# Two DMA queues for the first weights, and own orders of work for the first two steps of a graph-network kernel

## The reference

```python
def layer(h, adj, Wl, bl, Ws, bs, Wr, br, g, beta):
    u = einsum('bid,bjd->bij', h, h) / sqrt(384)
    delta = softmax(u) * adj
    attn = delta / (sum(delta, -1) + 1e-10)
    ctx = (attn above diagonal) @ (h @ Wl.T + bl) \
        + diag(attn) * (h @ Ws.T + bs) \
        + (attn below diagonal) @ (h @ Wr.T + br)
    return relu(layernorm(ctx, eps=1e-12) * g + beta)

h = relu(layernorm(x, 1e-5)); x = x + layer2(layer1(h))   # L0: two sublayers
h = relu(layernorm(x, 1e-5)); x = x + layer3(h)           # L1
```

## Time and profile before

| | us |
|---|---|
| median of 3 runs | 1231.8 (1230.98 to 1233.81) |
| the profiled execution | 1233.29 |
| its span | 1231.5 |
| TensorE busy | 1215.2 |
| VectorE busy | 1089.2 |
| ScalarE busy | 833.1 |
| GpSimd busy | 326.8 |

### The profile page before, as it was taken

The page is one execution under the profiler, slowest core; times in us unless marked ns, Lnnn a source line. Parts: engine busy times, 40 slices in busy tenths (PEclk is TensorE's granted clock), DMA queues, the critical chain, the costliest instruction groups (busy, mean ns, idle before and its releaser), DMA issues.

```text
span 1231.5 us, 26747 instructions
## 1 busy us (share of the span) xinstructions
PE 1215.2 (99%) x7163; PEld 1208.6 (98%) x7163; DVE 1089.2 (88%) x3127; ACT 833.1 (68%) x2079; POOL 326.8 (27%) x439
## 2 busy tenths in 40 slices
PE   7899999999999999999999999999999999999997
PEld 6899999999999999999999999999999999999997
DVE  6799888888887799999999999999999999999986
ACT  6577767666666667776766666676666666676764
POOL 1234232222222123321212121232323232323221
PEclk9999999999999999999999999999999999999999
DMA  5444232324232234333333323322332323232321
GB/s 179 135 121 129 89 114 83 118 82 119 83 106 91 94 99 130 116 100 104 96 106 96 107 85 103 129 85 95 97 107 98 106 95 99 96 97 98 99 91 54
DMA packets 112922, 127.18 MB, mean 103 GB/s; under 512 B 11104, under 2 KB 100192, under 8 KB 112864
## 3 DMA queue, kind: packets, MB, share of 16 engines
q1 hardware_dynamic: 112864, 126.50, 32.8%
HBM read 76.91 MB, written 49.55 MB: 103 GB/s over the span
## 4 chain that ended last, share of the span: by engine, by line
PE 97%; DMA 1%; issue 1%; DVE 1%; SPq 0%; ACT 0%; POOLq 0%; POOL 0%; DVEq 0%; ACTq 0%
PE right_bank L448 25%; PE left_bank L448 24%; PE context_bank L448 24%; PE context_bank L479 17%; PE score_bank L423 6%; PE score_bank L431 1%; DMA rows<-weights 1%; DMA nodes<-squares 0%; PE edge_bank L438 0%; ACT side_parts L610 0%; DVE context L872 0%; SPq L340 0%; DVE rows L881 0%; DVE stats L844 0%; DVE turned L744 0%
## 5 line engine op out<-in xcount | busy, mean ns | idle before, releaser
L448 PE MATMUL left_bank<-weight,node_t 128*128 128x384 f32 x1728 | 338.1, 339 | 0.0
L448 PE MATMUL right_bank<-weight,node_t 128*128 128x384 f32 x1728 | 335.0, 338 | 2.2 <-DVE weight L827 2.2
L448 PE MATMUL context_bank<-weight,node_t 128*128 128x384 f32 x1728 | 332.3, 337 | 3.1 <-ACT context_bank L616 3.1
L610 ACT ACTIVATE side_parts<-right_bank 128x384 fp32r<-128x384 f32 x192 | 94.4, 492 | 317.3 <-PE context_bank L479 317.1
L448 PEld LDWEIGHTS context_bank<-weight,node_t 128*128 128x128 f32 x1728 | 303.0, 188 | 3.7 <-ACT context_bank L616 3.4
L448 PEld LDWEIGHTS left_bank<-weight,node_t 128*128 128x128 f32 x1728 | 304.3, 188 | 0.0
L448 PEld LDWEIGHTS right_bank<-weight,node_t 128*128 128x128 f32 x1728 | 299.4, 188 | 3.5 <-issue 2.6
L479 PE MATMUL context_bank<-side_parts,attn_t 128*128 128x386 f32 x1152 | 240.0, 344 | 2.2 <-issue 1.9
L479 PEld LDWEIGHTS context_bank<-side_parts,attn_t 128*128 128x128 f32 x1152 | 198.9, 189 | 4.5 <-issue 3.6
L748 DVE TENSOR_TENSOR node_t<-nodes,node_t 128x768 fp32r<-128x768 f32 x94 | 121.6, 1294 | 18.2 <-ACT node_t L558 18.2
L1034 POOL TENSOR_TENSOR edge_block<-edge,tri 128x512 f32<-128x512 f32 x96 | 131.9, 1374 | 0.0
(11 more groups left out here) (78 smaller groups left out, 1519.6 us busy)
## 6 DMA issues: line engine op xcount, KB each, us to landing
squares<-turned SPq DMA_DIRECT2D x94, 384.0 KB, 2.7
nodes<-squares SPq DMA_DIRECT2D x376, 96.0 KB, 2.2
rows<-x SPq DMA_DIRECT2D x64, 384.0 KB, 3.7
out<-rows SPq DMA_DIRECT2D x31, 384.0 KB, 2.6
adj_in<-adj SPq DMA_DIRECT2D x96, 64.0 KB, 1.9
piece<-weights SPq DMA_DIRECT2D x18, 192.0 KB, 2.5
rows<-weights SPq DMA_DIRECT2D x3, 576.0 KB, 8.5
vector_rows<-vectors SPq DMA_DIRECT2D x3, 384.0 KB, 5.3
```

The source lines that it names most:

```text
L448: mm = nc.tensor.matmul(bank[:, 0:D], node_t[:, s.parity, k, c, a], weight[:, s.phase % 2, w, c, b], start=False, stop=(c, a) == (CH - 1, ...
L610: nc.scalar.activation(side_parts[:, side, HI, 0:D], side_bank[side][k][:, 0:D], ACT.Copy).then_inc(side_hi[side], 1)
```

## The change

SP no longer loads the RIGHT and LEFT weights and biases. ScalarE's queue does, ahead of ScalarE's first computation: the second tile of x(0), chunk 0 of the RIGHT weights with a semaphore of its own, the RIGHT bias, chunks 1 and 2, the LEFT weights, the LEFT bias. SP loads the first tile of x(0), the identity, x(1), the SELF weights, x(2), adj(0), the triangles, the SELF bias. Chunk 0 of RIGHT is split ahead of the first fill_source and input_shift. right(0,0) waits for the low part of tile 0 alone (`first_split`). The fillers are five and five.

In step 0, ScalarE does scale_self, seed_self and copy_cross ahead of the fills; VectorE does context_stats, denominator and sum_scores ahead of turn_nodes(2), and turn_nodes(3) behind centre. Step 1 gets orders of its own on TensorE, ScalarE and VectorE: TensorE does scores(2) after left(1,1) and not after self(1,0); ScalarE does split_nodes(2) after the seeds; VectorE does split_nodes(2) after the norms and turn_nodes(4) after centre(1,0). Step 2 on stays as `body`.

```diff
...
         first_bias_in = [sem("first_left_bias_in"), sem("first_right_bias_in"), sem("first_self_bias_in")]
+        first_x_in = sem("first_x_in")
+        first_chunk_in = sem("first_chunk_in")
...
         first_rounded = sem("first_rounded")
+        first_split = sem("first_split")
...
-            def load_first(w):
-                sp.dma_start(first_raw[:, w * CH:(w + 1) * CH], weights[0, w * CH:(w + 1) * CH].rearrange("c p e -> p c e"))\
-                  .then_inc(first_in[w], 16)
-            def load_first_bias(w):
-                sp.dma_start(vector_row(0, ROW_LEFT + w), vectors[0, ROW_LEFT + w].partition_broadcast(P)).then_inc(first_bias_in[w], 16)
-            load_x(Step(0, 0, 0))
+            sp.dma_start(rows[:, 0], x_pairs[0, :, 0]).then_inc(first_x_in, 16)
             sp.dma_start(context[:, 0, 0:P], identity).then_inc(identity_in, 16)
             load_x(Step(0, 0, 1))
-            for w in (RIGHT, LEFT):
-                load_first_bias(w)
-                load_first(w)
+            sp.dma_start(first_raw[:, SELF * CH:(SELF + 1) * CH], weights[0, SELF * CH:(SELF + 1) * CH].rearrange("c p e -> p c e"))\
+              .then_inc(first_in[SELF], 16)
+            load_x(Step(0, 1, 0))
             load_adj(Step(0, 0, 0))
             sp.dma_start(tri[:, :, :], triangles).then_inc(triangles_in, 16)
-            load_x(Step(0, 1, 0))
-            load_first(SELF)
-            load_first_bias(SELF)
+            sp.dma_start(vector_row(0, ROW_SELF), vectors[0, ROW_SELF].partition_broadcast(P)).then_inc(first_bias_in[SELF], 16)
...
             def project_side(s, k, side, within=None):
-                pe.wait_ge(node_hi, s.n + 1)
-                pe.wait_ge(node_lo, s.n + 1)
+                if isinstance(s.n, int) and (s.n, k, side) == (0, 0, RIGHT):
+                    pe.wait_ge(first_split, 1)
+                else:
+                    pe.wait_ge(node_hi, s.n + 1)
+                    pe.wait_ge(node_lo, s.n + 1)
...
+            def second_step(s):
+                prev, nxt = s.ahead(-1), s.ahead(1)
+                project_side(s, 0, RIGHT)
+                weigh(prev, 1)
+                project_side(s, 0, LEFT)
+                project_self(s, 0)
+                project_side(s, 1, RIGHT)
+                project_side(s, 1, LEFT)
+                scores(nxt)
+                weigh(s, 0)
+                project_self(s, 1, within=lambda: turn_cross(nxt))
             def body(s):
                 if isinstance(s.n, int) and s.n == 0:
                     return first_step(s)
+                if isinstance(s.n, int) and s.n == 1:
+                    return second_step(s)
...
             mm.then_inc(banks_open, 1)
-            keep_busy(3)
+            keep_busy(5)
             pe.wait_ge(ident_rounded, 1)
             start = Step(0, 0, 0)
             transpose_first(start)
-            keep_busy(6)
+            keep_busy(5)
...
-            def split_first(w):
-                act.wait_ge(first_in[w], 16)
-                for i in range(w * CH, (w + 1) * CH):
-                    nc.scalar.activation(piece_part(0, i, HI), first_raw[:, i], ACT.Copy).then_inc(first_hi[w], 1)
+            def split_first(w, chunks=range(CH)):
+                for i in chunks:
+                    act.wait_ge(first_chunk_in if (w, i) == (RIGHT, 0) else first_in[w], 16)
+                    nc.scalar.activation(piece_part(0, w * CH + i, HI), first_raw[:, w * CH + i], ACT.Copy).then_inc(first_hi[w], 1)
+            def load_first(w, chunks, arrived):
+                n = slice(w * CH + chunks[0], w * CH + chunks[-1] + 1)
+                act.dma_start(first_raw[:, n], weights[0, n].rearrange("c p e -> p c e")).then_inc(arrived, 16)
+            def load_first_bias(w):
+                act.dma_start(vector_row(0, ROW_LEFT + w), vectors[0, ROW_LEFT + w].partition_broadcast(P)).then_inc(first_bias_in[w], 16)
...
                 split_edges(s)
+                scale_self(s, 0)
+                seed_self(s, 1)
+                copy_cross(nxt)
+                seed_side(nxt, 0, RIGHT)
                 fill_source(second, 0)
                 fill_source(second, 1)
+                split_side(s, 1, RIGHT)
+                split_side(s, 1, LEFT)
+                scale_self(s, 1)
+                seed_side(nxt, 0, LEFT)
+                exponentials(nxt)
+                fill_source(third, 0)
+                fill_source(third, 1)
+            def second_step(s):
+                nxt, third = s.ahead(1), s.ahead(3)
+                split_side(s, 0, RIGHT)
+                seed_self(s, 0)
+                split_edges(s)
+                split_side(s, 0, LEFT)
+                seed_side(s, 1, RIGHT)
                 scale_self(s, 0)
+                seed_side(s, 1, LEFT)
                 seed_self(s, 1)
+                split_nodes(nxt)
...
                 scale_self(s, 1)
+                exponentials(nxt)
                 seed_side(nxt, 0, LEFT)
-                exponentials(nxt)
...
                     return first_step(s)
+                if isinstance(s.n, int) and s.n == 1:
+                    return second_step(s)
...
+            act.dma_start(rows[:, 1], x_pairs[0, :, 1]).then_inc(x_in[0], 16)
+            load_first(RIGHT, (0,), first_chunk_in)
+            load_first_bias(RIGHT)
+            load_first(RIGHT, (1, 2), first_in[RIGHT])
+            load_first(LEFT, (0, 1, 2), first_in[LEFT])
+            load_first_bias(LEFT)
             act.wait_ge(identity_in, 16)
             nc.scalar.activation(ident_r[:, :], context[:, 0, 0:P], ACT.Copy).then_inc(ident_rounded, 1)
             start = Step(0, 0, 0)
+            split_first(RIGHT, (0,))
             fill_source(start, 0)
...
             split_first_nodes(start)
-            split_first(RIGHT)
+            split_first(RIGHT, (1, 2))
...
-                if s.phase == 0:
+                if isinstance(s.n, int) and (s.n, k) == (0, 0):
+                    dve.wait_ge(first_x_in, 16)
+                elif s.phase == 0:
...
                                                  node_t[:, s.parity, k, :, HI].bitcast(F32), ALU.subtract)
-                mm.then_inc(node_lo, 1)
+                    mm.then_inc(first_split if k == 0 else node_lo, 1)
...
-            def split_first(w):
-                for i in range(CH):
+            def split_first(w, chunks=range(CH)):
+                for i in chunks:
...
                 gather_stats(third)
+                context_stats(s, 0)
+                denominator(s, 0)
+                sum_scores(nxt)
                 turn_nodes(second)
...
                 split_side(s, 1, LEFT)
-                sum_scores(nxt)
-                context_stats(s, 0)
-                denominator(s, 0)
-                turn_nodes(third)
                 gather_moments(s, 0)
                 mask_edges(nxt)
                 centre(s, 0)
+                turn_nodes(third)
                 gather_stats(fourth)
                 input_shift(fourth)
+            def second_step(s):
+                prev, nxt, third, fourth = s.ahead(-1), s.ahead(1), s.ahead(3), s.ahead(4)
+                diagonal(s)
+                context_stats(prev, 1)
+                denominator(prev, 1)
+                split_side(s, 0, RIGHT)
+                gather_moments(prev, 1)
+                squared_denominator(prev)
+                spreads(prev)
+                split_side(s, 0, LEFT)
+                split_edges(s)
+                centre(prev, 1)
+                input_stats(fourth, 0)
+                input_stats(fourth, 1)
+                norm(prev, 0)
+                norm(prev, 1)
+                gather_input(fourth, 0)
+                gather_input(fourth, 1)
+                split_nodes(nxt)
+                input_shift(fourth)
+                context_stats(s, 0)
+                denominator(s, 0)
+                split_side(s, 1, RIGHT)
+                split_side(s, 1, LEFT)
+                gather_moments(s, 0)
+                sum_scores(nxt)
+                centre(s, 0)
+                turn_nodes(third)
+                mask_edges(nxt)
...
                     return first_step(s)
+                if isinstance(s.n, int) and s.n == 1:
+                    return second_step(s)
...
             gather_stats(start)
+            split_first(RIGHT, (0,))
             input_shift(start)
             gather_stats(start.ahead(1))
             split_first_nodes(start)
+            split_first(RIGHT, (1, 2))
             input_shift(start.ahead(1))
-            split_first(RIGHT)
```

## The result

| | before | changed | |
|---|---|---|---|
| median of the runs | 1231.39 us | 1247.0 us (1246.14 to 1247.86) | ratio 1.0121, 95% interval 1.0109 to 1.0134 |
| profiled execution | 1233.29 us | 1246.14 us | +12.85 |
| its span | 1231.5 us | 1244.3 us | +12.8 |

The median of before is that of four runs here; the three known to the prediction had 1231.8. The prediction said slower, 1238.3 us, and at most 1242.5. The direction and the places were right, the size was not: +6.5 us against +12.85 in the profiled executions and +15.6 between the medians.

The account below looks back on a forecast made before the run. TensorE, busy 1215.2 of 1231.5 us, was taken as the bound. Loads 0.5, step 2 stall 4.2, clock 1.4 and RIGHT seed 0.4 gave +6.5 us, forecast 1238.3 us from a 1231.8 median, range 1234.5 to 1242.5.

Parts of the forecast that it names:

- both bounds: Start of the kernel: the changed loads lose 1.9 us or win up to 2 us; +0.5 us was taken.
- equal turns: Loads: the two queues alternate, so the LEFT bias lands at 15.9, 5.1 us later, and 1.9 us are lost.
- the walk: Step-by-step reckoning through steps 0 to 2, starting with weigh(0,0) at 24.46, the loads' term left out.
- the other bound: Loads: slow stretch overlaps the second queue, clock stays full, RIGHT starts 1.5 us sooner; up to 2 us won.
- VectorE in step 0 and the wait for scores(2): Steps 0 and 1: later turn_nodes(2) delays read_squares(2), and split_nodes(2) comes late; TensorE idles 4.9 us before scores(2).
- The stall of step 2: Ahead of self(2,0): late turn_nodes(4) delays read_squares(3); a 3.4 us wait, self(2,0) at 54.3 instead of 50.05, +4.2 us.
- X: Step 1: the time split_nodes(2) ends on VectorE, put at 43.0, from which scores(2) and step 2 are counted.
- The clock: Half clock after the idle before scores(2), +1.4 of at most 1.7 us; a second stretch at step 2 taken as 0.
- no wait for the RIGHT seed: Step 2: the forecast had seeding RIGHT (2,1) behind the fills add 0.4 us.
- VectorE keeps up: Rival: VectorE reaches split_nodes(2) before nodes(2) lands, ending before about 38.8; 1229.2 us, chance 0.18.
- the loads win: Rival: start wins 1.5 to 2 us, x(5) in time, clock full, orders lose less; 1233.2 us, chance 0.14.
- Equal turns and a second slow clock: Rival: loads lose by alternating queues and a second half-clock stretch comes; +9.6 us, 1241.4 us, chance 0.13.

Follow-up runs that it names:

- e8: e2 with SP holding back the SELF weights and all behind them until the LEFT weights are in; 1233.39 us against 1231.87 before, ratio 1.0009.
- e1: The changed kernel with VectorE's input_shift(5) moved to the end of step 1; 1243.32 us against 1233.13 before, ratio 1.0083.
- e9: The changed kernel with ScalarE's two fill_source(4) directly behind split_nodes(2) in step 1; 1244.37 us against 1232.13 before, ratio 1.0100.
- e10: e9 with VectorE's turn_nodes(4) directly behind split_nodes(2); 1238.55 us against 1232.13 before, ratio 1.0053.
- e2: The kernel before with only the changed loads, early chunk 0 and fillers; 1236.33 us against 1233.13 before, ratio 1.0033.
- a2: The changed kernel itself, run again on another chip; 1246.73 us against 1232.13 before, ratio 1.0121.
- e3: The kernel before with only the changed orders of steps 0 and 1, its prologue kept; 1241.51 us against 1233.13 before, ratio 1.0073.
- e6: The kernel before with e5's line and other step 1 orders on TensorE, ScalarE and VectorE; 1227.4 us against 1231.87 before, ratio 0.9961.
- e5: The kernel before with ScalarE's scale_self(0,0) moved ahead of the two fill_source(2) in step 0; 1231.26 us against 1231.87 before, ratio 0.9992.
- e12: e6 with nine fillers instead of six behind the first transposes; 1228.1 us against 1232.13 before, ratio 0.9966.

## Why the prediction was wrong in size

**The loads.** I had both bounds and chose +0.5 us between them; the trace took the upper one and more. The left seed came at 15.99 (15.9 by equal turns), left(0,0) at 18.26 (18.0), weigh(0,0) 2.4 us behind the 24.46 of the walk. The reasons I gave for the other bound did not hold. The slow stretch stayed: 161 GB/s from 4 to 6 us in the changed kernel, 147 before. RIGHT started 0.5 us sooner and not 1.5, and the clock was at 0.50 from 14 to 16 us as before. e8 shows that the bytes ahead make the bias late. The Trainium skill ("DMA: Bandwidth & Descriptors", "Issuing engines are not separate DMA queues") says that DMAs of several engines run on the same 16 DMA engines and interleave. The trace agrees: the 15.99 is where equal turns of the two queues had put the seed.

**VectorE in step 0 and the wait for scores(2).** Right in kind and close in size: turn_nodes(2) 3.20 us behind weigh(0,0) (worked out: 3.19), TensorE idle 4.1 us ahead of scores(2) (4.9), scores(2) 17.3 us behind weigh(0,0) (18.5). The write of the squares took 2.3 us and not 3.2, and left(1,1) waited 0.4 us and not 1.4.

**The stall of step 2: here the step failed.** I wrote that VectorE gets to sum_scores(2) at X + 3.8 and ends turn_nodes(4) at X + 5.9. It got there at X + 8.2 and X + 10.3, counted from the start of scores(2), 44.17. I had moved input_shift(5) along with VectorE's list and put its wait at nothing, without a reason; in the trace of before it ran without one (45.34). But GpSimd's input_rstd(5) overwrites what fill_source(4) reads, and so waits for it; and the new order put fill_source(4) behind split_side(1,1) on ScalarE, hence behind weigh(1,0) on TensorE. So VectorE waited for GpSimd, GpSimd for ScalarE and ScalarE for TensorE, 6.69 us in all. In e1, where context_stats(1,0) does not stand behind that wait, it starts 3.28 us behind scores(2) and not 6.67: 3.4 us of the 6.69 lay on the path, and of the 4.4 us by which sum_scores(2) was late. The other 1.0 us is there in e1 too, where scores(2) and weigh(1,0) also ran at half clock, which the sum had as a term of its own. e1 takes VectorE's link out of the chain, e9 the one between ScalarE and TensorE, and each brings context_stats(1,0) to directly behind weigh(1,0). I had counted every instruction of the moved steps, but not the waits of the engine that feeds them.

The rest of the place was right: e10 shows that with an early turn_nodes(4) the wait before self(2,0) is gone.

**The clock.** One stretch of half clock was in the sum and came. The second, which I took as 0 of 1.7 us, came too: self(2,0) took 3.25 us.

The sum of 6.5 us, put right by what was measured: loads +1.9 (2.4 and not 0.5), scores(2) sooner -1.2, the wait of input_shift(5) +3.4, a slower read and smaller differences behind it +0.6, second stretch +1.7 (the upper bound of the prediction, not measured by itself), no wait for the RIGHT seed -0.4. That is 6.5 + 6.0 = 12.5 us of the 12.85 between the profiled executions. The 15.6 us between the medians contain 1.9 us by which the profiled execution of before was slower than its median, and 0.9 by which that of the changed kernel was faster. With every term at its upper bound the prediction's own sum was +9.9 us, 1241.7: even the 12.85 us lie above all of it, mainly because the wait of input_shift(5) had no term.

Of the rivals, "VectorE keeps up" fell (split_nodes(2) ended at 44.07, 38.8 was its limit), as did "the loads win". "Equal turns and a second slow clock" was the nearest, at a chance of 0.13, and still 3 us short of the profiled difference for want of this wait.

## What to carry to other kernels

When an instruction is moved in a list written by hand, follow its inputs through every engine to the point where they are released, not only to the engine that delivers them: a wait that the trace shows at zero can be zero only because of the order. A DMA round trip through a single buffer has to be started as early as its inputs allow; a later start moved the stall of 3.1 us to the next step here and made it longer. A second DMA queue did not bring its bytes sooner while the first was given other work at the same time (the left seed at 15.31 in e2, at 12.52 in e8, at 12.09 with one queue).

## What the runs showed that I had not expected

The four reads of read_squares took SP 1.75 us to issue in most places, but 2.94 us at 54.54 in the changed kernel, so that the last one started 1.2 us late. The same read_squares(3) took 2.79 us in a2, 2.55 in e1, 2.71 in e3 and 2.67 in e9; at 47.49 in e10 it was 1.75 again, while e6 had 2.30 for read_squares(2). No run tells why.

One line's place (e5) or three more fillers (e12) changed nothing that can be told from noise, while the start of the same prologue differed by a microsecond between kernels: right(0,0) began at 12.09 in the kernel before and at 11.09 in e3, whose prologue is the same.
